# Two routed layers of a fused network: routes copied by DMA, shared rows first, an eviction moved, gating in smaller portions

## The chip, the cores and the metric

The kernel runs on 1 core of one Trainium2 chip. Its time is the device time of one execution in microseconds (us), the median of several runs. Five engines work side by side, each through its own queue in order: TensorE (PE; its weight loads are PEld), VectorE (DVE), ScalarE (ACT), GpSimd (POOL) and SyncE (SP, which here only issues DMAs). They wait for each other by semaphores.

## The reference

x is 16 batches x 256 tokens x 128 channels in float32, and passes through four pairs of sublayers, each added to its input: a cross attention and a feed-forward network, layers 0 to 3. Only two feed-forward networks change. With x normalised over its channels:

```python
# layer 1: 8 experts of 176 hidden units, the best 2 by score, and one shared expert
scores = softmax(x @ gate_w.T); idx = top_k(scores + gate_b, 2)
rw = zeros(T, 8).at[idx].add(scores[idx])
h  = silu((x @ w1[e] + b1[e]) * (x @ w3[e] + b3[e]))          # for each expert e
y  = sum_e rw[e] * (h @ w2[e] + b2[e])  +  the same of the shared expert, unweighted

# layer 2: 16 experts, all computed, weights rw from a gating with a softmax over the positive logits
q, k, v = (sum_e rw[e] * (x @ proj[e]) for the three projections)
ao  = softmax(causal(q @ k.T / sqrt(128))) @ v
out = sum_e rw[e] * (ao @ o_proj[e])
```

## The kernel before

The 4096 tokens lie in SBUF as x_sb. Each sublayer is a block with a barrier at its end. A feed-forward block runs 8 iterations (ITERS) of 512 tokens (T4); the first and last two are written out, the middle ones are a hardware loop of two iterations. Within a block the order of each engine's work is written out by hand; what an iteration prepares for the next (normalisation, transposes, gating: the functions named front_...) stands at fixed steps between the main work.

**Layer 1 (layer1_ffn).** The nine experts' 9 x 176 = 1584 hidden rows lie one behind the other and are cut into 13 chunks (CH) of 128 rows, the last of 48. At step k TensorE does the six one-pass matmuls of the next chunk (up, L1446; two products, each in three high and low parts), then front work, then the output matmul of the chunk two steps back (down, L1462, float32, two records), then spread (L1452): a bf16 matmul of a 0/1 matrix selb with the transposed routes rwTb, which puts into the psR bank the route of each hidden row. ScalarE adds a bias (L1380) and applies silu (L1386); VectorE multiplies the two products (L1567) and multiplies by psR (weigh, L1574). The biases of the output come by a separate matmul with the routes in float32 (L1460). For it the routes, with a constant 1 for the shared expert, are split by VectorE into three parts (three_parts, L1107 to L1112), transposed by TensorE (L1436) at step 11 and copied twice by ScalarE (L1374, L1375). No DMA is issued in this block. At its head GpSimd fills two tiles (L1355, L1356), for which VectorE and TensorE wait.

**Layer 2 (layer2_ffn).** The routes go to memory and come back spread over all partitions by DMA (L1733, L1739), four experts to a group. An iteration j (main) has 16 steps, one per expert: VectorE scales x by the route (L2037), ScalarE makes a rounded high part (xsh, L1809), VectorE the low part (xsl, L2041), TensorE nine matmuls (L1925). A ring of four tiles links them. Then come the attention and, mixed into it, 16 output matmuls (mix_o, L1913) for iteration j - 1. At the end of main ScalarE evicts their sum (store_o, L1804) and only then turns to the first high part of the next iteration. The gating of the next iteration is done by VectorE at steps 6 to 9 and 11, ScalarE's exponential stands at step 10, the transposed output (out_T) at 10, its addition at 12, the transposes of the routes (L1867) on TensorE at 14 and their copy (L1798) on ScalarE after step 15. In the first iteration the attention runs without output matmuls. In what follows a "seam" is the passage from one iteration to the next.

The order on ScalarE at the end of an iteration (store_o waits for the last output matmul) and at the start of the next:

```python
                if has_second_next(j):
                    front_squares(j + 2)
                if not is_first(j, 1):
                    store_o(j)
...
                    act.wait_ge(s("scaled").sem, s("scaled").at(qn(j, e + 1)))
                    nc.scalar.activation(xsh[:, e % RING, :], xs[:, e % RING, :], ACT.Copy)
```

## Time and profile before

| | |
|---|---|
| median of 3 runs | 1762.16 us (1762.01 to 1770.39) |
| the profiled execution | 1769.78 us, span 1767.8 us |
| busy share of the span | PE 86%, PEld 59%, DVE 69%, ACT 50%, POOL 10% |
| granted TensorE clock, mean | 0.945 of full speed |
| layer 1's feed-forward block | 436 to 740 us |
| layer 2's feed-forward block | 916 to 1440 us |
| DMA | 108 MB, 61 GB/s over the span |

One execution was profiled, on its only core. A line of the trace gives the start and the length of an instruction in us, its engine, its line in the kernel, its tiles and, in brackets, how long the engine was idle before it and what released it. Matmuls are pipelined: a record of 0.4 us may start every 0.23 us, so the distance between starts counts. Some matmul records are missing. Records of the same group that follow each other are merged (x14). PEclk is the clock that the throttle granted, 1.00 being 2.4 GHz.

### The profile page before, as it was taken

How to read it: one execution, taken by the hardware profiler on the slowest of the kernel's cores; microseconds unless marked ns; L12 is line 12 of the kernel's file. 1: busy time of each engine (PE TensorE's matmuls, PEld its weight loads, DVE VectorE, ACT ScalarE, POOL GpSimd, SP SyncE). 2: the span in 40 equal slices, each digit the busy share in tenths (PEclk: the TensorE clock that was granted, in tenths of full speed). 3: DMA queues.
4: the chain of work that ended last, by engine and by line, in shares of the span. 5: the costliest groups of instructions: out<-in, count | busy, mean ns of one | idle time of the engine just before them, and what ended most of it. 6: DMA issues, size and time to landing. Idle time of an engine off the chain costs nothing. (4 is left out here: it accounts for less than half of the span.)

```text
span 1767.8 us, 24778 instructions
## 1 busy us (share of the span) xinstructions
PE 1516.7 (86%) x8181; PEld 1038.8 (59%) x8201; DVE 1217.6 (69%) x2650; ACT 883.5 (50%) x1583; POOL 178.4 (10%) x171
## 2 busy tenths in 40 slices
PE   6999988896899999988966899999999988979407
PEld 5777765554566666566644656656656745655206
DVE  3888965786676676556656576767666557877896
ACT  2656644774556555465632333232233227756893
POOL 2111011130000000111410000000000011121000
PEclk9999999999899999999987999999999999999758
DMA  4000001320000000051202342433244312100001
GB/s 170 1 1 1 0 1 37 116 55 19 1 0 1 0 0 1 9 171 49 59 8 96 136 151 108 156 144 134 105 167 167 123 64 70 50 24 1 1 0 48
DMA packets 33708, 108.03 MB, mean 61 GB/s; under 512 B 8957, under 2 KB 12413, under 8 KB 24638
## 3 DMA queue, kind: packets, MB, share of 16 engines
q1 hardware_dynamic: 33598, 106.64, 17.9%
q8 instruction: 59, 0.97, 0.2%
q14 instruction: 51, 0.42, 0.1%
HBM read 85.38 MB, written 2.36 MB: 50 GB/s over the span
## 5 line engine op out<-in xcount | busy, mean ns | idle before, releaser
L1016 DVE TENSOR_REDUCE mP_a<-psY_a 128x8 f32<-128x512 f32 x192 | 128.1, 688 | 102.1 <-PE psY_a L842 102.0
L760 ACT ACTIVATE probs_a<-psX_a 128x512 f32<-128x512 f32 x192 | 109.0, 595 | 129.1 <-PE psX_a L869 128.3
L1809 ACT ACTIVATE xsh_f<-xs_f 128x512 fp32r<-128x512 f32 x128 | 79.4, 630 | 166.8 <-DVE xs_f L2037 166.8
L1567 DVE SCALAR_TENSOR_TENSOR g_f<-psU_f,cols_f1w,t_f 128x512 f32<-128x512 f32 (+1 forms) x104 | 77.9, 749 | 72.8 <-ACT t_f L1380 71.0
L1913 PE MATMUL psX_f<-xs_f,wo_f2w 128*128 128x512 f32 x256 | 121.3, 606 | 2.1 <-DVE xs_f L2037 1.5
L1380 ACT ACTIVATE t_f<-psU_f,cols_f1w 128x512 f32<-128x512 f32 (+1 forms) x104 | 71.1, 684 | 76.2 <-PE psU_f L1446 76.2
L1462 PE MATMUL psO_f<-h_f,w_f1w 128*128 128x512 f32 (+1 forms) x208 | 107.6, 599 | 0.0
L2041 DVE TENSOR_TENSOR xsl_f<-xs_f,xsh_f 128x512 fp32r<-128x512 f32 x128 | 87.8, 686 | 16.0 <-ACT xsh_f L1809 14.9
L842 PE MATMUL psY_a<-ks_a,xs_a 96*128 96x256 f32 x384 | 94.7, 348 | 4.1 <-DMA xs_a<-ql_a 2.4
L869 PE MATMUL psX_a<-xs_a,ks_a 128*128 128x256 f32 x384 | 86.2, 325 | 13.3 <-ACT xs_a L749 13.3
L1023 DVE RECIPROCAL heads_a<-psV_a 128x256 f32<-128x256 f32 x48 | 83.9, 1748 | 8.8 <-PE psV_a L882 8.8
L1925 PE MATMUL psQ_f<-xsh_f,wql_f2w 128*128 128x512 f32 x128 | 58.8, 459 | 35.1 <-DVE xsl_f L2041 34.7
L2268 PE MATMUL ps_f<-sel 128*128 128x512 f32 x76 | 23.1, 452 | 72.4 <-DVE gt_f L2495 72.4
L842 PEld LDWEIGHTS psY_a<-ks_a,xs_a 96*128 96x128 f32 x384 | 64.2, 199 | 34.2 <-DVE mP_a L1016 22.8
L869 PEld LDWEIGHTS psX_a<-xs_a,ks_a 128*128 128x128 f32 x384 | 63.4, 195 | 28.0 <-ACT xs_a L749 24.6
L1574 DVE TENSOR_TENSOR h_f<-act_h_f,psR_f 128x512 f32<-128x512 f32 (+1 forms) x104 | 70.5, 678 | 13.5 <-ACT act_h_f L1386 8.7
L183 POOL TENSOR_TENSOR rstd_f<-vareps_f,mhalf 128x4 f32<-128x4 f32 x16 | 18.1, 1133 | 562.1 <-DVE vareps_f L169 562.1
L1913 PEld LDWEIGHTS psX_f<-xs_f,wo_f2w 128*128 128x128 f32 x256 | 45.0, 192 | 48.8 <-issue 29.9
L1386 ACT ACTIVATE act_h_f<-g_f 128x512 f32<-128x512 f32 (+1 forms) x104 | 65.0, 625 | 3.2 <-DVE g_f L1567 3.1
L469 PE MATMUL psC_a<-vhat_a,pT_a 128*128 128x128 f32 x512 | 63.2, 277 | 0.5 <-DVE x_sb L546 0.5
L469 PEld LDWEIGHTS psC_a<-vhat_a,pT_a 128*128 128x128 f32 x512 | 61.2, 194 | 1.3 <-issue 0.6
L2268 PEld LDWEIGHTS ps_f<-sel 128*128 128x128 f32 x76 | 15.9, 221 | 76.4 <-issue 73.2
(444 smaller groups left out, 3969.5 us busy)
## 6 DMA issues: line engine op xcount, KB each, us to landing
wq_f2w<-f_routes SPq DMA_DIRECT2D x16, 1024.0 KB, 4.6
wk_f2w<-f_routes SPq DMA_DIRECT2D x16, 1024.0 KB, 4.7
wv_f2w<-f_routes SPq DMA_DIRECT2D x16, 1024.0 KB, 4.7
ring_f2w<-f_routes SPq DMA_DIRECT2D x16, 1024.0 KB, 4.8
xs_a<-qh_a SPq DMA_DIRECT2D x168, 64.0 KB, 2.0
xs_a<-ql_a SPq DMA_DIRECT2D x84, 64.0 KB, 2.0
xs_a<-probs_a SPq DMA_DIRECT2D x36, 64.0 KB, 2.0
x_sb<-in_x SPq DMA_DIRECT2D x1, 2048.0 KB, 8.0
```

Source lines behind the costliest of these rows:

```text
L469: ins = nc.tensor.matmul(psC[:, 0:P], pT[:, g % 2, k * P:(k + 1) * P], vhat[:, g // TPI % 2, g % TPI // 2, k, :], start=k == 0, stop=k == ...
L760: nc.scalar.activation(probs[:, b % 2, g, :, :], psX[g % 2][:].rearrange("p (e t) -> p e t", e=2), ACT.Exp, scale=float(dv) ** -0.5).then_ ...
L842: ins = nc.tensor.matmul(psY[h % 2][:, e * GK:(e + 1) * GK], xs[0:MAXROW, j % 2, g, t:t + P], ks[0:MAXROW, j % 2, p, g, :], start=not mask ...
L869: ins = nc.tensor.matmul(psX[g % 2][:, e * ST:(e + 1) * ST], ks[:, j % 2, p, g, e * P:(e + 1) * P], xs[:, j % 2, g, p * ST:(p + 1) * ST], ...
L1016: nc.vector.tensor_reduce(mP[:, b % 2, h // 2, col:col + 8], psY[h % 2][:].rearrange("p (h k) -> p h k", h=8), axis=AX.X, op=ALU.max).then ...
L1023: nc.vector.reciprocal(heads[:, b % 2, :], psV[:, ST:2 * ST]).then_inc(s("sums_inverted").sem, 1)
L1380: nc.scalar.activation(t3[r, g % 2, :], psU[g % 2][r, 1, :], ACT.Identity, bias=cols[r, CH + g % CH:CH + g % CH + 1])\
L1462: ins = nc.tensor.matmul(psO[:], w2[0:rows[k], k, :], h[0:rows[k], g % 2, :], start=False, stop=k == CH - 1)
L1567: nc.vector.scalar_tensor_tensor(g_[r, g % 2, :], psU[g % 2][r, 0, :], cols[r, k:k + 1], t3[r, g % 2, :], ALU.add, ALU.mult).then_inc(s("h ...
L1809: nc.scalar.activation(xsh[:, e % RING, :], xs[:, e % RING, :], ACT.Copy).then_inc(s("x_high").sem, 1)
L1913: nc.tensor.matmul(psX[:], wo[:, e, :], xs[:, e % RING, :], start=e == 0, stop=e == E - 1)\
L2041: nc.vector.tensor_tensor(xsl[:, e % RING, :], xs[:, e % RING, :], xsh[:, e % RING, :], ALU.subtract)\
```

## The change

Layer 1. The 176 shared rows come first, as chunks of 128 and 48 rows (L1_ROUTED = 2), which need no route; 8 chunks of 128 rows of one expert each follow, and 3 chunks with 16 rows of each of the 8 experts. The selection matrix, its conversion to bf16 at the end of the attention before, the spread matmuls and the psR banks go. The route of each row comes from memory: SyncE writes the transposed routes and reads them back into spread0, spread1 (four experts each, over all partitions) and spread2 (16 partitions for each expert). The output biases become rows 64 to 72 of chunk 1's weights, and the routes rows 64 to 72 of its right side hs, so the bias matmul and the split into three parts go. The transposes of the routes move from step 11 to 10.

Layer 2. store_o moves behind the high parts of experts 0 and 1 of the next iteration; the gating goes from steps 6 to 9 and 11 to steps 7 to 11 and 13, one of its portions cut in two; the exponential moves from 10 to 12, out_T from 10 to 12, the addition from 12 to 14, the transposes of the routes from 14 to 15. Filler matmuls (keep_busy, one pass, 512 columns, from the constant sel into psX) are added in the prologue and between the parts of the first attention.

The diff, without the semaphores' counts and the host's reordering of the weights:

```diff
@@ -1291,49 +1291,60 @@
...
+L1_ROUTED = 2
+L1_BIAS_ROW = 64
...
+def layer1_rows():
...
+    first = [(L1_E, h) for h in range(L1_H)]
+    whole = [(e, h) for e in range(L1_E) for h in range(P)]
+    rest = [(e, P + 16 * c + i) for c in range(3) for e in range(L1_E) for i in range(16)]
+    return first + whole + rest
...
 def layer1_ffn(pr, x_sb, common, wt):
...
     T4 = TPI * P
+    routes = nc.dram_tensor("f1_routes", (ITERS, E * T4), F32).ap()
...
         top, gs = sb("top", [P, TPI]), sb("gs", [P, TPI])
-        rw, rest = sb("rw", [P, TPI, NE]), sb("rest", [P, TPI, NE])
-        hi, mid = sb("hi", [P, TPI, NE], BF16), sb("mid", [P, TPI, NE], BF16)
-        parts = sb("parts", [P, TPI, P])
-        rwT, rwTb = sb("rwT", [P, 2, T4]), sb("rwTb", [P, 2, T4], BF16)
+        rw, hs = sb("rw", [P, TPI, P]), sb("hs", [P, 2, T4])
+        spread = [sb("spread0", [P, 4 * T4]), sb("spread1", [P, 4 * T4]), sb("spread2", [P, T4])]
+        biases = slice(L1_BIAS_ROW, L1_BIAS_ROW + NE)
...
         psU = [ctx.enter_context(nc.psum_tensor(f"psU{k}_f1", [P, 2, T4], F32)) for k in range(2)]
-        psR = [ctx.enter_context(nc.psum_tensor(f"psR{k}_f1", [P, T4], F32)) for k in range(2)]
...
         psM = ctx.enter_context(nc.psum_tensor("psM_f1", [P, T4], F32))
-        NST = LN_STEPS + 1 + 1 + 1 + 1 + 1 + 5 + 1 + 5 + 1 + 1 + 3
-        rows = [min(P, L1_ALL - k * P) for k in range(CH)]
+        NST = LN_STEPS + 1 + 1 + 1 + 1 + 1 + 5 + 1 + 5 + 1
+        rows = [P, L1_H - P] + [P] * (CH - L1_ROUTED)
+        starts = [sum(rows[:k]) for k in range(CH)]
+        RC = CH - L1_ROUTED
...
@@ -1350,10 +1361,30 @@
+        @block.sync
+        def _(sp):
+            for j in range(ITERS):
+                sp.wait_ge(s("gate_parts").sem, s("gate_parts").at(j + 1))
+                sp.dma_start(routes[j].rearrange("(e t) -> e t", e=E), hs[L1_BIAS_ROW:L1_BIAS_ROW + E, j % 2, :])\
+                    .then_inc(s("routes_kept").sem, 16)
+                sp.wait_ge(s("routes_kept").sem, s("routes_kept").at(16 * (j + 1)))
+                for half in range(2):
+                    if j:
+                        sp.wait_ge(s("hidden_ready").sem, s("hidden_ready").at(RC * (j - 1) + 4 * (half + 1)))
+                    sp.dma_start(spread[half][:], routes[j, half * 4 * T4:(half + 1) * 4 * T4].partition_broadcast(P))\
+                        .then_inc(s(f"spread{half}").sem, 16)
+                if j:
+                    sp.wait_ge(s("hidden_ready").sem, s("hidden_ready").at(RC * j))
+                for e in range(E):
+                    sp.dma_start(spread[2][e * 16:(e + 1) * 16, :], routes[j, e * T4:(e + 1) * T4].partition_broadcast(16))\
+                        .then_inc(s("spread2").sem, 16)
...
         def _(pool):
-            nc.gpsimd.memset(rw[:], 1.0).then_inc(s("pool_steps").sem, 1)
-            nc.gpsimd.memset(parts[:], 0.0).then_inc(s("pool_steps").sem, 1)
+            nc.gpsimd.memset(rw[:], 0.0).then_inc(s("pool_steps").sem, 1)
+            nc.gpsimd.memset(hs[:], 0.0).then_inc(s("pool_steps").sem, 1)
+            pool.wait_ge(s("pool_steps").sem, s("pool_steps").at(2))
+            nc.gpsimd.memset(rw[:, :, L1_BIAS_ROW + E:L1_BIAS_ROW + NE], 1.0).then_inc(s("pool_steps").sem, 1)
...
@@ -1371,8 +1402,7 @@
                 act.wait_ge(s("gate_T").sem, s("gate_T").at(j + 1))
-                nc.scalar.activation(rwT[:, q, :], psM[:], ACT.Copy)
-                nc.scalar.activation(rwTb[:, q, :], psM[:], ACT.Copy).then_inc(s("gate_parts").sem, 1)
+                nc.scalar.activation(hs[biases, q, :], psM[biases, :], ACT.Copy).then_inc(s("gate_parts").sem, 1)
...
@@ -1381,12 +1411,15 @@
             def silu(n, g):
-                r = slice(0, rows[g % CH])
+                r, k = slice(0, rows[g % CH]), g % CH
                 act.wait_ge(s("hidden_mul").sem, s("hidden_mul").at(n + 1))
-                nc.scalar.activation(act_h[r, g % 2, :], g_[r, g % 2, :], ACT.Silu).then_inc(s("hidden_act").sem, 1)
+                if k < L1_ROUTED:
+                    act.wait_ge(s("hidden_down").sem, s("hidden_down").at(n - 1))
+                kept = (h[r, g % 2, :], hs[r, g // CH % 2, :])[k] if k < L1_ROUTED else act_h[r, g % 2, :]
+                nc.scalar.activation(kept, g_[r, g % 2, :], ACT.Silu).then_inc(s("hidden_act").sem, 1)
...
             def store_out(j):
-                act.wait_ge(s("ffn_out").sem, s("ffn_out").at(j + 1))
+                act.wait_ge(s("hidden_down").sem, s("hidden_down").at((j + 1) * CH))
...
@@ -1405,8 +1438,9 @@
                                 front_exp(j + 1)
-                            if k == 11:
+                            if k == 10:
                                 front_parts(j + 1, 1 - p)
+            act.wait_ge(s("pool_steps").sem, s("pool_steps").at(3))
...
@@ -1433,12 +1467,12 @@
                 for c in range(TPI):
-                    ins = nc.tensor.transpose(psM[:, c * P:(c + 1) * P], parts[:, c, :], ident[:])
+                    ins = nc.tensor.transpose(psM[:, c * P:(c + 1) * P], rw[:, c, :], ident[:])
...
                 k, q = g % CH, g // CH % 2
-                cs, r = slice(k * P, k * P + rows[k]), slice(0, rows[k])
+                cs, r = slice(starts[k], starts[k] + rows[k]), slice(0, rows[k])
...
@@ -1446,22 +1480,19 @@
-            def spread(n, g):
-                k, q = g % CH, g // CH
-                pe.wait_ge(s("hidden_ready").sem, s("hidden_ready").at(n - 1))
-                nc.tensor.matmul(psR[g % 2][0:rows[k], :], selb[:, k * P:k * P + rows[k]], rwTb[:, q, :], start=True, stop=True)\
-                    .then_inc(s("gate_bcast").sem, 1)
...
                 if k == 0:
...
                     pe.wait_ge(s("ffn_outT").sem, s("ffn_outT").at(j))
-                    nc.tensor.matmul(psO[:], b2[:], rwT[:, q, :], start=True, stop=False)
-                pe.wait_ge(s("hidden_ready").sem, s("hidden_ready").at(n + 1))
-                ins = nc.tensor.matmul(psO[:], w2[0:rows[k], k, :], h[0:rows[k], g % 2, :], start=False, stop=k == CH - 1)
-                if k == CH - 1:
-                    ins.then_inc(s("ffn_out").sem, 1)
+                if k == 1:
+                    pe.wait_ge(s("gate_parts").sem, s("gate_parts").at(j + 1))
+                if k < L1_ROUTED:
+                    pe.wait_ge(s("hidden_act").sem, s("hidden_act").at(n + 1))
+                else:
+                    pe.wait_ge(s("hidden_ready").sem, s("hidden_ready").at(RC * j + k - L1_ROUTED + 1))
+                r = slice(0, L1_BIAS_ROW + NE if k == 1 else P)
+                rhs = hs[r, q, :] if k == 1 else h[r, g % 2, :]
+                nc.tensor.matmul(psO[:], w2[r, k, :], rhs, start=k == 0, stop=k == CH - 1).then_inc(s("hidden_down").sem, 1)
...
@@ -1489,15 +1520,12 @@
                             out_T(j - 1)
-                        if front and k == 11:
+                        if front and k == 10:
...
                             down(n - 2, (g - 2) % BODY, j - 1 if k < 2 else j)
-                        if k == 0:
-                            pe.wait_ge(s("gate_parts").sem, s("gate_parts").at(j + 1))
-                        spread(n, g)
...
@@ -1556,8 +1584,7 @@
                 steps.done(nc.vector.tensor_tensor(oh[:], oh[:], oh2[:], ALU.add))
-                steps.done(nc.vector.tensor_tensor(rw[:, :, 0:E], oh[:], ex[:], ALU.mult))
-                three_parts(nc, steps, rw[:], parts[:], hi[:], rest[:], mid[:], NE).then_inc(s("gate_ready").sem, 1)
+                nc.vector.tensor_tensor(rw[:, :, L1_BIAS_ROW:L1_BIAS_ROW + E], oh[:], ex[:], ALU.mult).then_inc(s("gate_ready").sem, 1)
...
@@ -1567,11 +1594,16 @@
-            def weigh(n, g):
-                r = slice(0, rows[g % CH])
+            def weigh(n, g, j):
+                c = g % CH - L1_ROUTED
+                if c < 0:
+                    return
+                if c in (0, 4, 8):
+                    dve.wait_ge(s(f"spread{c // 4}").sem, s(f"spread{c // 4}").at((16 * E if c >= 8 else 16) * (j + 1)))
                 dve.wait_ge(s("hidden_act").sem, s("hidden_act").at(n + 1))
-                dve.wait_ge(s("gate_bcast").sem, s("gate_bcast").at(n + 1))
-                nc.vector.tensor_tensor(h[r, g % 2, :], act_h[r, g % 2, :], psR[g % 2][r, :], ALU.mult)\
+                dve.wait_ge(s("hidden_down").sem, s("hidden_down").at(n - 1))
+                weights = spread[2][:] if c >= 8 else spread[c // 4][:, c % 4 * T4:(c % 4 + 1) * T4]
+                nc.vector.tensor_tensor(h[:, g % 2, :], act_h[:, g % 2, :], weights, ALU.mult)\
...
@@ -1589,7 +1621,7 @@
                         if g or not first:
-                            weigh(n - 1, (g - 1) % BODY)
+                            weigh(n - 1, (g - 1) % BODY, j if k else j - 1)
...
@@ -1807,10 +1840,12 @@
                     nc.scalar.activation(xsh[:, e % RING, :], xs[:, e % RING, :], ACT.Copy).then_inc(s("x_high").sem, 1)
+                    if e == 1 and not is_first(j, 2):
+                        store_o(j - 1)
...
                             front_x(j + 1, 1 - q)
-                        elif e == 10:
+                        elif e == 12:
...
@@ -1833,14 +1868,13 @@
                     front_squares(j + 2)
-                if not is_first(j, 1):
-                    store_o(j)
...
             run_mains(act, main)
+            store_o(ITERS - 1)
...
@@ -1926,7 +1960,7 @@
                         pe.wait_ge(s("ao_ready").sem, s("ao_ready").at(j))
-                    if e == 10 and not is_first(j, 2):
+                    if e == 12 and not is_first(j, 2):
...
@@ -1935,7 +1969,7 @@
                             front_logits(j + 1, 1 - q)
-                        elif e == 14:
+                        elif e == 15:
...
@@ -1946,13 +1980,25 @@
                 if is_first(j, 1):
+                    keep_busy(8)
...
                         stage()
+                        keep_busy(6)
+                    keep_busy(14)
...
                     mix_o(j, stages)
...
+            def keep_busy(n):
...
+                for _ in range(n):
+                    nc.tensor.matmul(psX[:], common["sel"][:, 0, :], common["sel"][:, 0:4, :], start=True, stop=True)
+            keep_busy(16)
             front_x(0)
+            keep_busy(4)
             front_logits(0, 0)
+            keep_busy(24)
             front_parts(0)
+            keep_busy(36)
...
@@ -2007,10 +2053,12 @@
-            def front_second(steps):
+            def front_inactive(steps):
...
                 steps.done(nc.vector.scalar_tensor_tensor(lg[:], oh[:], -1e30, lg[:], ALU.mult, ALU.add))
...
+            def front_second(steps):
...
@@ -2075,19 +2123,21 @@
                         low_part(E * j + e - 1, e - 1)
-                    if e == 12 and not is_first(j, 2):
+                    if e == 14 and not is_first(j, 2):
...
                     if not is_last(j):
-                        if e == 6:
+                        if e == 7:
...
                             front_gate(j + 1, steps)
-                        elif e == 7:
+                        elif e == 8:
                             front_best(steps)
-                        elif e == 8:
+                        elif e == 9:
+                            front_inactive(steps)
+                        elif e == 10:
                             front_second(steps)
-                        elif e == 9:
+                        elif e == 11:
                             front_mask(steps)
-                        elif e == 11:
+                        elif e == 13:
```

## Rows read from the trace of the kernel before

**Rows 1.** busy time by stretch; per engine, PEclk, DMA share, GB/s

```profile
438.00:740.00 302.00, 292.26 (x1092) 183.05 (x1112) 201.77 (x531) 166.93 (x271) 8.06 (x8) 0.97 0.00 1
```

**Rows 2.** in order of time (start us, us, engine, line), ScalarE, two evictions

```profile
564.40 0.60 ACT L1391 ACTIVATE oT_f<-psO_f 128x512 f32<-128x512 f32 x1 [2.41 <-PE psO_f L1462]
...
600.44 0.60 ACT L1391 ACTIVATE oT_f<-psO_f 128x512 f32<-128x512 f32 x1 [2.40 <-PE psO_f L1462]
```

**Rows 3.** in order of time, TensorE, one chunk

```profile
576.28 0.38 PE L1452 MATMUL psR_f<-rwTb_f,selb_f1w 128*128 128x512 bf16 x1
...
576.73 0.39 PE L1446 MATMUL psU_f<-xl_f,w3h_f1w 128*128 128x512 f32 x1
...
576.96 0.39 PE L1446 MATMUL psU_f<-xh_f,w3h_f1w 128*128 128x512 f32 x1
...
578.74 0.38 PE L1452 MATMUL psR_f<-rwTb_f,selb_f1w 128*128 128x512 bf16 x1
```

**Rows 4.** in order of time, TensorE, chunk 0 of an iteration

```profile
566.27 1.02 PE L1460 MATMUL psO_f<-rwT_f,b_f1w 128*128 128x512 f32 x2
...
567.13 1.02 PE L1462 MATMUL psO_f<-h_f,w_f1w 128*128 128x512 f32 x2
```

**Rows 5.** in order of time, VectorE, the gating stretch, one iteration

```profile
578.74 0.69 DVE L1574 TENSOR_TENSOR h_f<-act_h_f,psR_f 128x512 f32<-128x512 f32 x1 [1.19 <-ACT act_h_f L1386]
...
587.78 0.18 DVE L1107 CAST hi_f<-rw_f 128x36 bf16<-128x36 f32 x1
...
588.73 0.75 DVE L1567 SCALAR_TENSOR_TENSOR g_f<-psU_f,cols_f1w,t_f 128x512 f32<-128x512 f32 x1
```

**Rows 6.** in order of time, the second layer's first routes, SyncE and VectorE

```profile
937.15 0.34 SPq L1733 DMA_DIRECT2D f_routes<-rwT_f  x1
...
943.06 1.29 DVE L2037 TENSOR_TENSOR xs_f<-xT_f,wq_f2w 128x512 f32<-128x512 f32 x2 [2.29 <-DMA wq_f2w<-f_routes]
```

**Rows 7.** in order of time, GpSimd, fills at the head of two stages

```profile
436.33 0.52 POOL L1356 MEMSET parts_f<- 128x512 f32 x1
...
740.57 0.95 POOL L688 MEMSET vs_a<- 128x1024 f32 x1
```

**Rows 8.** in order of time, the seam from second to third iteration, four engines

```profile
1050.84 6.17 PE L1913 MATMUL psX_f<-xs_f,wo_f2w 128*128 128x512 f32 x14
...
1055.09 1.29 DVE L2037 TENSOR_TENSOR xs_f<-xT_f,wq_f2w 128x512 f32<-128x512 f32 x2
...
1057.05 0.60 ACT L1804 ACTIVATE oT_f<-psX_f 128x512 f32<-128x512 f32 x1 [2.67 <-PE psX_f L1913]
...
1058.94 0.50 PE L1925 MATMUL psQ_f<-xsh_f,wql_f2w 128*128 128x512 f32 x1 [1.93 <-DVE xsl_f L2041]
```

**Rows 9.** in order of time, VectorE, the loop's back edge

```profile
1178.85 1.29 DVE L2037 TENSOR_TENSOR xs_f<-xT_f,wq_f2w 128x512 f32<-128x512 f32 x2 [2.71 <-PE psX_f L1913]
```

**Rows 10.** in order of time, TensorE, first three experts after a later seam

```profile
1242.23 0.69 PE L1925 MATMUL psQ_f<-xsh_f,wql_f2w 128*128 128x512 f32 x1 [2.01 <-DVE xsl_f L2041]
...
1245.98 0.40 PE L1925 MATMUL psQ_f<-xsh_f,wql_f2w 128*128 128x512 f32 x1
...
1248.08 0.40 PE L1925 MATMUL psQ_f<-xsh_f,wql_f2w 128*128 128x512 f32 x1
```

**Rows 11.** in order of time, TensorE, starts of experts 5 and 10

```profile
1070.79 0.48 PE L1925 MATMUL psQ_f<-xsh_f,wql_f2w 128*128 128x512 f32 x1
...
1083.34 0.40 PE L1925 MATMUL psQ_f<-xsh_f,wql_f2w 128*128 128x512 f32 x1
```

**Rows 12.** in order of time, ScalarE, the end of an iteration's experts

```profile
1035.57 0.59 ACT L1798 ACTIVATE rwT_f<-psM_f 16x512 f32<-16x512 f32 x1 [5.38 <-PE psM_f L1867]
...
1037.67 0.60 ACT L1818 ACTIVATE qkvT_f<-psQ_f 128x512 f32<-128x512 f32 x1 [1.51 <-PE psQ_f L1925]
```

**Rows 13.** busy time by stretch, two stretches of the second layer

```profile
945.20:948.90 3.70, 3.62 (x9) 2.88 (x10) 2.34 (x4) 1.26 (x2) 0.00 (x0) 0.51 1.00 421
...
997.60:1003.30 5.70, 5.68 (x13) 4.46 (x14) 3.57 (x6) 1.89 (x3) 0.00 (x0) 0.50 0.48 187
```

More of the change, by code:

```diff
@@ L2107, in _ @@
             front_best(steps)
+            front_inactive(steps)
             front_second(steps)
@@ L2651, in joined @@
         return np.concatenate([a, b[None]], axis=0)
+    experts, places = np.array(layer1_rows()).T
     def chunked(a):
         out = np.zeros((L1_CH * P, a.shape[1]), a.dtype)
[L2655 to L2656 removed]
+        out[:L1_H] = a[:L1_H]
+        out[L1_ROUTED * P:] = a[L1_H:]
+        return out
     for k in ("w1", "w3"):
[L2659 to L2661 removed]
+        d["F1_" + k] = np.ascontiguousarray(joined(f["L1_ffn_" + k], f["L1_ffn_s" + k])[experts, :, places].T)
+    w2 = chunked(joined(f["L1_ffn_w2"], f["L1_ffn_sw2"])[experts, places])
+    w2[P + L1_BIAS_ROW:P + L1_BIAS_ROW + L1_E + 1] = joined(f["L1_ffn_b2"], f["L1_ffn_sb2"])
+    d["F1_w2"] = rows(w2)
+    d["F1_cols"] = np.concatenate([rows(chunked(joined(f["L1_ffn_" + k], f["L1_ffn_s" + k])[experts, places][:, None]))[:, :, 0]
                                    for k in ("b1", "b3")], axis=1)
[L2663 to L2666 removed]
     d["F1_gw"], d["F1_gb"] = f["L1_ffn_gate_w"].T, f["L1_ffn_gate_b"]
[L2668 removed]
     d["desc16"] = np.arange(L2_E, 0, -1).astype(np.float32)
```

31 lines of the change are left out of this document (11 added, 20 removed).

## The prediction

> **What bounds the kernel now.** I read the table by stretch of time first, then the instructions in order of time of one iteration on each engine, then the waits at the seams. The first routed layer runs from 438 to 740 us. In it TensorE is busy 292 of 302 us at a mean granted clock of 0.97 of 2.4 GHz [rows 1]; the reader is to see that no other engine comes near this. Its period is 600.44 - 564.40 = 36.04 us per iteration [rows 2], 13 chunks each. So here a matmul taken away is time taken away, as long as VectorE keeps up. The second routed layer (916 to about 1440 us) is bound by TensorE inside its loops over 16 experts but stands still at seams: at the change from one iteration to the next, and in the stretch where VectorE does the gating. The rest of the kernel isn't touched, apart from a weight conversion on ScalarE behind work that VectorE still does.
>
> **First layer, what goes from TensorE.** The one-pass bf16 matmul that spreads a route goes, 13 per iteration. Its price is its slot in the stream, not its duration: from it to the second matmul of the next chunk is 576.73 - 576.28 = 0.45 us, a plain one takes 576.96 - 576.73 = 0.23, so its slot is 0.22 of the chunk's 578.74 - 576.28 = 2.46 us [rows 3]. 13 x 0.22 = 2.9 us. The separate bias matmul goes too: 567.13 - 566.27 = 0.86 us [rows 4]; its rows now ride in the chunk of the last 48 shared hidden rows, and that matmul has 512 columns whatever its rows. Together 3.7 us per iteration, 30 us over 8.
>
> Does VectorE keep up? It loses two of 13 multiplications by the route (0.68 each) and the three-part split, 588.73 - 587.78 = 0.95 us [rows 5]. It is unbroken from the multiplication at 578.74 on, and the matmuls of chunk 11 wait a little for it (about 0.3 us, twice). I set up the new iteration, with chunks 2.24 us apart: VectorE then ends the product of chunk 9 some 15.7 us after the start of chunk 5's matmuls, TensorE is there at 15.1. So one stall of 0.6 us where there are now three of about 0.2; net nothing. The transposes of the routes, now one step earlier (10 for 11), need the routes at that time + 1.5 and VectorE has them at + 1.0. The new waits: a multiplication by the route waits for the down matmul two chunks back; the product before it on VectorE ends about 0.7 us after that matmul, so this wait is covered, and was already there through the spread matmul. ScalarE's silu of chunk 1 waits for the last down matmul of the iteration before, some 0.2 us; queued behind it are the two copies of the next x, with 2 us to spare.
>
> **First layer, what is added.** One write of the routes to memory and 10 reads per iteration on SyncE's queue, which was empty in this layer. The same pair in the second layer takes 943.06 - 937.15 = 5.9 us from issue of the write to the first product with it [rows 6]. Here routes are on their way some 12 us before chunk 2 needs them (5 chunks of 2.24 us), so 6 us are to spare; the reads of the third piece (8 issues) have over 15 us. In the first iteration there is no lead: 5.9 us against some 8 us until chunk 2's product, which nothing covers if it is late, worth 0 to 2 us once; I take 0. At the head of the layer VectorE waits for three fills in place of two. 128x512 takes 0.52 us, 128x1024 0.95 [rows 7]; so 0.46 + 0.95 + 0.15 in place of 0.55, +1.0 us. Against this the split (0.95) and one of two copies on ScalarE (0.5) go from the same serial head: -0.5 in all. First layer: -30.5 us, bounds -20 (a stall of 1.3 us more per iteration) and -34 (all present stalls go).
>
> **Second layer, the output's eviction.** At a seam the last output matmul is issued until about 1056.9; ScalarE has waited for it and evicts at 1057.05, only then makes the high part of the first scaled x, VectorE the low part, and TensorE starts at 1058.94 after 1.93 us. Yet the scaled x was there at 1055.78 [rows 8]. With the eviction behind two high parts: high part 55.8 to 56.45, low part to 57.15, start at 57.2. That is 1.7 us less. There are 6 such seams (the first iteration has no output to evict, the last eviction stands after the loop as before); but at the loop's back edge VectorE itself comes only at 1178.85, after 2.7 us [rows 9], so that seam gains nothing: 5 x 1.7 = 8.5 us. What is late next is the last output matmul itself.
>
> The seams have a second price. After such an idle time the first expert takes 1245.98 - 1242.23 = 3.75 us where the next takes 2.10 [rows 10]: the granted clock has gone to its lower level, 1.2 GHz, with some 1.5 us lost. I found this at five of the six seams, one of them the back edge. With 0.3 us of idle time in place of 2 the clock should hold at the four others, 6 us at most, 0 at least; I take 4.
>
> **Second layer, gating in smaller portions.** From expert 5 to expert 10 the matmuls take 1083.34 - 1070.79 = 12.55 us in place of 5 x 2.10 = 10.5 [rows 11]: VectorE has 1.3 to 1.95 us of gating beside 1.2 us of its own per expert, more than 2.10 in two of them, and begins it by waiting for the logits. Begun one expert later, VectorE is an expert ahead when it waits, and no portion is over 1.3 us; by my sum it stays 0.5 to 1 us ahead of TensorE throughout. 2.0 us gone, 7 times (the last iteration has no gating to do). The addition, now at 14, keeps its stall of about 0.2. A price comes with it: the routes' transposes go behind expert 15's matmuls, so ScalarE copies them (0.49 between starts) after these and not 2.1 us before the q, k, v evictions [rows 12]. TensorE waits for that copy before the output matmuls, and scores wait for the evictions: +0.4 us. Net -1.6 x 7 = -11, bounds -6 and -14. SyncE's write of the routes is 0.8 us later, its reads have several us left.
>
> **Second layer, filler matmuls.** They show nowhere in this place in the trace, so both ends from rows. The granted clock is 0.51 in the first 3.7 us of the first iteration, and 0.50 for 5.7 us after the 5.6 us of idle time that follow the first attention [rows 13]. At the upper level a filler takes 0.23 us: 16 + 4 + 24 + 36 of them fit the waits within half a us each, and give back 1.8 us (9 matmuls, 0.2 each) and about 0.5 in the transposes. After the first attention, 8 + 5 x 6 + 14 delay the next iteration by 3.0 us (it could start at 997.6, the fillers and the chain through them end at about 1000.6) and give back 14 x 0.2 = 2.8. Sum: -2. At the lower level, 0.43 us each, the prologue is 14 us longer and the attention 13 more, +27 for the other end. I take -2: the engine is busy without a gap before each group but the first.
>
> **Sum.** Against the profiled run's own 1769.8 us (span 1767.8): -30.5 - 8.5 - 4 - 11 - 2 = -56, so 1714. That run lies 7.6 us above the median of the runs, 1762.2; the removed slots are the same in both, so I forecast 1762 - 56 = 1706 us.
>
> **Rivals.** (1) VectorE becomes the bound of the first layer's gating stretch. For: it has 12 us there without a gap [rows 5]. Against: it loses 0.95 + 0.68 of them. Costs 1.3 us x 8 = 10: 1716.
> (2) The fillers run at the lower clock, for the reason that the first of them start cold: +27 + 2, so 1735. Against: the clock rose in under 6 us of matmuls each time in [rows 10, 13].
> (3) The clock falls in the first layer's loop, where 0.6 us of idle time per iteration are now in one place. For: it falls after the seams. Against: 0.6 is a third of a seam's idle time, and at 36 us periods with three small stalls it held. Once per iteration at a seam's price, 8 x 1.5 = 12: 1718.
> The Trainium skill, TensorE: Matmul & The Clock Gate, section "A second HAM failure mode: psum-queue depth-cycling", says that frequent micro-idles between groups of matmuls that cycle through PSUM banks make the clock oscillate; this loop is of that kind. The trace of before doesn't bear it out for this layer, whose mean is 0.97 with its cold head included [rows 1]; hence the low chance of (3).
> (4) Slower than before: the spread routes arrive late in each iteration of the first layer, since SyncE serves write, two large and eight small reads in order and each waits for buffers to come free. VectorE stands at chunk 2, behind it the next product, behind that TensorE. Price: what the load takes over its 12 us of lead, x 8. It decides from 7 us of wait per iteration, a load of 19 us against 5.9 measured [rows 6]; with 8 us of wait, 1706 + 64 = 1770.
> (5) The layers gain nothing, as the freed slots are filled by another wait: 1762. Against it stands [rows 2, 3]: 13 x 2.46 plus the extra groups is the whole period.
>
> **How the numbers follow.** Forecast 0.66, (1) 0.14, (2) 0.07, (3) 0.06, (4) 0.04, (5) 0.03. The forecast's own range is 1698 to 1716. With (1), (3) and part of (2), and below it the upper bounds of the first layer (-3.5), the clock (-2) and the gating (-3) and some more for the 8 us by which runs differ, 1690 to 1726. About 0.5% (9 us) is what a measurement of this kernel can tell: faster 0.93, same 0.03, slower 0.04.
>
> **What would show it.** Right: eviction period in the first layer 32.3 us (+-0.5); no wait on SyncE's reads beyond the first iteration; second-layer seams of 0.3 us but one of 3; starts of experts 5 to 10 in 10.6 us; filler spacing 0.23. Wrong: VectorE waiting for a DMA at chunk 2, a granted clock under 0.95 between 460 and 700 us, filler spacing of 0.43, or a first-layer period over 33.5.

## The result

| | before | after |
|---|---|---|
| median of the runs, us | 1764.97 (4 runs, 1762.01 to 1770.39) | 1713.51 (4 runs, 1709.67 to 1718.13) |
| profiled run, its own time / span, us | 1769.78 / 1767.8 | 1713.01 / 1710.9 |
| ratio of the times | | 0.9691 [0.9664, 0.9719] |

The kernel is 3.1% faster. The forecast was 1714 us for the profiled run (measured 1713.0) and 1706 for the median (measured 1713.5, inside the range).

### The profile page after: what moved, and what is told of

Its sections match the earlier page's. It is cut to its first block and busy times, and to the rows that moved or that the text cites. A ratio compares the mean times of both kernels' runs of the same rounds, so it can differ in the third digit from the quotient of the medians.

```text
span 1710.9 us, 24871 instructions
## 1 busy us (share of the span) xinstructions
PE 1494.7 (87%) x8213; PEld 1042.7 (61%) x8213; DVE 1201.3 (70%) x2586; ACT 880.9 (51%) x1574; POOL 179.5 (10%) x172
## 5 line engine op out<-in xcount | busy, mean ns | idle before, releaser
L1594 DVE SCALAR_TENSOR_TENSOR g_f<-psU_f,cols_f1w,t_f 128x512 f32<-128x512 f32 (+1 forms) x104 | 78.0, 750 | 61.1 <-ACT t_f L1410 59.3
L1495 PE MATMUL psO_f<-h_f,w_f1w 128*128 128x512 f32 x192 | 98.4, 595 | 0.4 <-DVE h_f L1606 0.4
L1410 ACT ACTIVATE t_f<-psU_f,cols_f1w 128x512 f32<-128x512 f32 (+1 forms) x104 | 71.2, 685 | 52.8 <-PE psU_f L1480 52.1
L842 PEld LDWEIGHTS psY_a<-ks_a,xs_a 96*128 96x128 f32 x384 | 64.1, 198 | 32.3 <-DVE mP_a L1016 22.8
L1480 PE MATMUL psU_f<-xh_f,w3l_f1w 128*128 128x512 f32 (+1 forms) x104 | 75.3, 724 | 6.0 <-DVE g_f L1594 5.9
L1606 DVE TENSOR_TENSOR h_f<-act_h_f,spread_f 128x512 f32<-128x512 f32 x88 | 60.1, 683 | 10.9 <-ACT act_h_f L1419 8.3
L454 PE MATMUL psS_a<-khat_a,xT_a 128*128 128x512 f32 x128 | 60.1, 593 | 0.7 <-ACT khat_a L378 0.7
```

The source lines that it names most:

```text
L842: ins = nc.tensor.matmul(psY[h % 2][:, e * GK:(e + 1) * GK], xs[0:MAXROW, j % 2, g, t:t + P], ks[0:MAXROW, j % 2, p, g, :], start=not mask ...
L1480: ins = nc.tensor.matmul(psU[g % 2][r, half, :], wt_part[:, cs], x_part[:, q, :], start=m == 0, stop=m == 2)
L1495: nc.tensor.matmul(psO[:], w2[r, k, :], rhs, start=k == 0, stop=k == CH - 1).then_inc(s("hidden_down").sem, 1)
L1594: nc.vector.scalar_tensor_tensor(g_[r, g % 2, :], psU[g % 2][r, 0, :], cols[r, k:k + 1], t3[r, g % 2, :], ALU.add, ALU.mult).then_inc(s("h ...
```

## The profile after

**First routed layer.** The same view as in [rows 1], for the block from its first instruction to its last output eviction and a little beyond (before: 436.28 to 738.40, 302.1 us). Columns as there: length, busy time and count for TensorE, its weight loads, VectorE, ScalarE and GpSimd, granted clock, DMA share, GB/s.

```profile
437.97:712.65 274.68, 258.68 (x989) 169.52 (x989) 186.06 (x471) 165.36 (x263) 9.59 (x11) 0.98 0.19 70
```

It is 27.4 us shorter. The period shows in ScalarE's two evictions that answer to [rows 2]: 555.05 - 522.34 = 32.71 us in place of 36.04.

```profile
522.34 0.60 ACT L1424 ACTIVATE oT_f<-psO_f 128x512 f32<-128x512 f32 x1 [1.70 <-PE psO_f L1495]
...
555.05 0.60 ACT L1424 ACTIVATE oT_f<-psO_f 128x512 f32<-128x512 f32 x1 [1.64 <-PE psO_f L1495]
```

One of TensorE's waits is new. The view of waits, TensorE, that block (before, the first line stood at 5.8 and the second at 0.5):

```profile
PE psM_f L1458 <- DVE xn_f L175: 6.4, 1, 6.4
PE psU_f L1480 <- DVE g_f L1594: 5.9, 8, 0.8
```

Where one of the eight stands is seen in order of time. VectorE begins behind ScalarE's silu, is unbroken through the gating up to the product of 542.18, and TensorE's up matmuls start 0.77 us late:

```profile
534.84 0.69 DVE L1606 TENSOR_TENSOR h_f<-act_h_f,spread_f 128x512 f32<-128x512 f32 x1 [1.19 <-ACT act_h_f L1419]
...
541.87 0.19 DVE L1101 TENSOR_TENSOR oh_f<-desc_f1w,top_f 128x32 f32<-128x32 f32 x1
542.18 0.75 DVE L1594 SCALAR_TENSOR_TENSOR g_f<-psU_f,cols_f1w,t_f 128x512 f32<-128x512 f32 x1
```

```profile
536.02 0.60 PE L1500 MATMUL psM_f<-ident,oT_f 128*128 128x128 f32 x4
...
537.23 0.50 PE L1480 MATMUL psU_f<-xh_f,w3l_f1w 128*128 128x512 f32 x1
...
539.70 0.50 PE L1480 MATMUL psU_f<-xh_f,w3l_f1w 128*128 128x512 f32 x1
...
542.99 0.50 PE L1480 MATMUL psU_f<-xh_f,w3l_f1w 128*128 128x512 f32 x1 [0.77 <-DVE g_f L1594]
```

The four steps from 534.23 to the start at 545.38 take 11.15 us. They hold four chunks of 2.25 and two groups of transposes of 0.44 (536.46 - 536.02), 9.88 us; 1.27 us are lost there, in each iteration of the loop. No wait of VectorE for a DMA stands in the block.

VectorE needs 542.18 - 534.84 = 7.34 us from the start of this stretch to that product. Before the change it was 586.07 - 578.74 = 7.33 us ([rows 5] has the start): the three-part split stood behind this product and the two multiplications that went stand in other chunks, so nothing that was removed lay in these 7.3 us.

```profile
586.07 0.75 DVE L1567 SCALAR_TENSOR_TENSOR g_f<-psU_f,cols_f1w,t_f 128x512 f32<-128x512 f32 x1
```

At the layer's head the three fills of GpSimd that answer to [rows 7] take 1.6 us, as worked out:

```profile
437.97 0.53 POOL L1384 MEMSET rw_f<- 128x512 f32 x1 [39.42 <-POOLq L617]
438.43 0.95 POOL L1385 MEMSET hs_f<- 128x1024 f32 x1
439.44 0.11 POOL L1387 MEMSET rw_f<- 128x4 f32 x1
```

**Second routed layer, a seam** (in order of time; it answers to [rows 8, 10]). The eviction now stands behind two high parts and TensorE waits 0.35 us, not 2.01. The first expert takes 1085.16 - 1082.96 = 2.20 us, so the clock held.

```profile
1082.72 0.60 ACT L1837 ACTIVATE oT_f<-psX_f 128x512 f32<-128x512 f32 x1
...
1082.96 0.50 PE L1959 MATMUL psQ_f<-xsh_f,wql_f2w 128*128 128x512 f32 x1 [0.35 <-DVE xsl_f L2089]
```

**The back edge** (it answers to [rows 9]). Still an idle time of 2.84 us, and yet the first expert takes 1144.29 - 1142.09 = 2.20 us. Before it took 3.71 here.

```profile
1142.09 0.50 PE L1959 MATMUL psQ_f<-xsh_f,wql_f2w 128*128 128x512 f32 x1 [2.84 <-DVE xsl_f L2089]
...
1144.29 0.40 PE L1959 MATMUL psQ_f<-xsh_f,wql_f2w 128*128 128x512 f32 x1
```

**Gating.** Experts 5 to 10 take 1048.76 - 1038.16 = 10.60 us in place of 12.55 [rows 11], and ahead of the output matmuls stands the new wait for ScalarE's copy of the routes (before, the scores waited 0.81 us at this point for an eviction, now 0.23):

```profile
1038.16 0.48 PE L1959 MATMUL psQ_f<-xsh_f,wql_f2w 128*128 128x512 f32 x1
...
1048.76 0.39 PE L1959 MATMUL psQ_f<-xsh_f,wql_f2w 128*128 128x512 f32 x1
...
1063.53 1.12 PE L1947 MATMUL psX_f<-xs_f,wo_f2w 128*128 128x512 f32 x2 [0.84 <-ACT rwT_f L1831]
1064.89 0.49 PE L1922 MATMUL psQ_f<-qkvT_f 128*128 128x128 f32 x2 [0.23 <-ACT qkvT_f L1855]
```

**Fillers.** The first 16 of the prologue take 5.59 us: the granted clock is 0.50 from 895 to 898 us and 0.97 from 898 to 901. The last 36 run at 0.23 us each, the 20 behind the first attention at 0.24, and iteration 1 starts warm (at the upper level) right behind them:

```profile
894.59 5.59 PE L1994 MATMUL psX_f<-sel 128*128 128x512 f32 x16 [3.46 <-DVE simn_f L2016]
...
908.77 8.43 PE L1994 MATMUL psX_f<-sel 128*128 128x512 f32 x36
...
966.10 4.82 PE L1994 MATMUL psX_f<-sel 128*128 128x512 f32 x20
970.75 0.40 PE L1959 MATMUL psQ_f<-xsh_f,wql_f2w 128*128 128x512 f32 x1
```

**Where the 56.9 us of the two spans went.** First layer -27.4. Second layer (its first matmul to the next stage's first: 917.50 to 1441.12 before, 890.74 to 1384.56 after) -29.8. The rest +0.3, in which +1.7 is the work ahead of the first layer: in its last 18 us the mean granted clock was 0.79 (before 1.00).

## The experiments

Times are medians; "before" is the kernel before, run on the same chip beside each group. In the traces the stretches agree from kernel to kernel to about 0.1 us, while the whole times of one kernel differ by up to 15 us, so the stretches decide and the times only confirm. "Cold" is a stretch that begins at the lower level of TensorE's clock, "warm" one that begins at the upper.

**1. First layer alone.** The second layer as before the change.

> The first routed layer as changed, the second as before. My theory: the first layer's block gives 302.1 - 274.7 = 27.4 us by itself, whatever the second does, and the second's seams have their cold first experts (3.3 to 3.8 us) and its period of 60 to 62 us back: 1762 - 27 = 1735 us, ratio to before 0.984. The rival, that part of the gain credited to the second layer comes from a warmer start after the first: 1730 or less, and the second layer's first main starts warm.

Measured 1742.05 us, before 1773.98, ratio 0.9814 [0.9766, 0.9862]. The evictions of the first layer come at 521.74 and 554.45, 32.71 us apart as in the changed kernel, to the hundredth, and the second layer has its old periods (52.1, 61.2, 59.8, 62.6, 61.1, 60.1, 61.0 us). The two layers' gains are separate, and the second's first iteration starts cold (3.58): the rival fell. Of the six seams three are cold, where the kernel before had five and the expectation all.

**2. No fillers.**

```
-            keep_busy(16)
             front_x(0)
-            keep_busy(4)
             ... (likewise 24, 36; in the first attention 8, 6 per stage, 14)
```

> All filler matmuls of the second layer left out (they compute nothing that is used), the rest as changed. Mine: they only pay where they stand. The first attention gets 3.0 to 3.9 us shorter, the first experts of iterations 0 and 1 take 3.8 again (+1.6 and +1.9) and the transposes and logits of the prologue some 1 us more: within +-2 us of the changed kernel, 1712 to 1716 us, and the later seams stay warm (2.2 us). Rival: the fillers are what set the clock for the loop behind them, and without them the seams are cold again: +7, 1720.

Measured 1713.26, before 1773.98, ratio 0.9669 [0.9612, 0.9725]. Prologue and first two periods together take 28.29 + 50.98 + 57.31 = 136.58 us, in the changed kernel 27.47 + 52.54 + 55.57 = 135.58: the fillers are worth 1.0 us. The seams behind them with 0.35 us of idle time stay at 2.20; only the back edge took 2.93. They pay only where they stand.

**3. Eviction back at the end of an iteration.**

```
-                    if e == 1 and not is_first(j, 2):
-                        store_o(j - 1)
...
+                if not is_first(j, 1):
+                    store_o(j)
```

> Only the output's eviction put back to the end of an iteration, gating portions and fillers as changed. Both theories: seams of 2 us idle again, 5 x 1.7 = 8.5 us. Mine as forecast: an idle time of 2 us at the seam is what lets the clock fall, so four or five first experts take 3.3 to 3.8 us again, +6: 1714 + 14 = 1728 us. Rival, from the back edge of the changed kernel, where the clock held through 2.84 us of idle time: the idle time at the seam does not decide, what went before it does (the stalls of the gating stretch); all first experts take 2.2, 1722 us.

Measured 1725.11 (1723.44 to 1726.15), before 1773.98, ratio 0.9716 [0.9667, 0.9764]. All seams stand idle for 1.93 to 2.10 us again. But of the five only one is cold, with 3.75 us; at the next, the same idle time costs nothing more (1089.22 - 1087.01 = 2.21):

```profile
1027.16 0.66 PE L1958 MATMUL psQ_f<-xsh_f,wql_f2w 128*128 128x512 f32 x1 [1.93 <-DVE xsl_f L2088]
...
1030.91 0.40 PE L1958 MATMUL psQ_f<-xsh_f,wql_f2w 128*128 128x512 f32 x1
...
1087.01 0.50 PE L1958 MATMUL psQ_f<-xsh_f,wql_f2w 128*128 128x512 f32 x1 [2.01 <-DVE xsl_f L2088]
...
1089.22 0.40 PE L1958 MATMUL psQ_f<-xsh_f,wql_f2w 128*128 128x512 f32 x1
```

The back edge is cold too (3.48). Neither theory has it whole: after an idle time of 2 us the clock falls or it doesn't. More on this below.

**4. Gating back in its larger portions.** In the second layer VectorE's steps at 6, 7, 8, 9, 11 in place of 7 to 11 and 13, exp and output transposes at 10, addition at 12, routes' transposes behind expert 14.

> Only the gating of the second layer put back into its larger portions, the routes' transposes one expert earlier and the addition at 12; eviction behind two high parts and fillers as changed. Mine: experts 5 to 10 take 12.5 us again (+2.0), the wait of 0.84 us for the copy of the routes goes: +1.3 x 7 = +9, and all seams stay warm, since their idle time is 0.3 us: 1723 us. Rival: the stalls in the gating stretch are what lets the clock fall at the seam or at the back edge: first experts of 3.3 to 3.8 us at up to six seams, +9 more, 1732.

Measured 1728.09, before 1773.98, ratio 0.9728 [0.9678, 0.9778]. Experts 5 to 10 take 12.35 to 12.84 us again; an undisturbed period is 58.15 us in place of 56.64, so the smaller portions with their price are worth 1.5 us there (forecast 1.6). Over the seven periods it is 0.9 to 1.8 us each: from the first start of iteration 0 to that of iteration 7 the two kernels take 404.69 and 393.03 us, and of these 11.66 us 1.55 are the cold back edge, so 10.1 us are the portions'. The five seams of at most 0.45 us stay warm, the back edge took 3.76.

**5. Routes' transposes behind expert 14**, otherwise as changed. One number in the code: `elif e == 15` is 14 on TensorE.

> The changed kernel with one line of the second layer changed: the routes' transposes stand behind expert 14's matmuls again. Mine: the wait of 0.84 us (0.68 in two iterations) for ScalarE's copy before the output matmuls goes, and nothing takes its place, since VectorE has added and weighted by expert 14: period 55.8 in place of 56.65, 7 x 0.85 = -6: 1708 us by the changed kernel's 1713.5. Rival: the transposes, one expert earlier, wait for VectorE's addition at 14 in turn, and the period stays within 0.3 of 56.65: 1713.

Measured 1711.46, before 1766.42, ratio 0.9678 [0.9656, 0.97]. A period falls to 56.10 us, by 0.55 and not 0.85: the wait of 0.84 for the copy is gone, but the scores wait 0.81 us for ScalarE's evictions again, in place of 0.23. These two waits alone would leave 0.26; where the other 0.3 us come from is not shown. And at two places the clock fell where it held in the changed kernel, after the same idle time: at the back edge (3.00 us), and in the last 32 output matmuls, 15.67 us in place of 13.97. First the kernel with the earlier transposes:

```profile
1138.40 0.50 PE L1959 MATMUL psQ_f<-xsh_f,wql_f2w 128*128 128x512 f32 x1 [2.84 <-DVE xsl_f L2089]
...
1141.40 0.63 PE L1959 MATMUL psQ_f<-xsh_f,wql_f2w 128*128 128x512 f32 x1
...
1364.41 15.67 PE L1947 MATMUL psX_f<-xs_f,wo_f2w 128*128 128x512 f32 x32 [1.54 <-DVE xs_f L2085]
```

and the changed kernel at the second of the two places:

```profile
1368.06 13.97 PE L1947 MATMUL psX_f<-xs_f,wo_f2w 128*128 128x512 f32 x32 [1.54 <-DVE xs_f L2085]
```

**6. First layer: output transposes and addition behind the gating.**

```
-                        if k == 7 and not (first and p == 0):     (TensorE, out_T)
+                        if k == 11 and not (first and p == 0):
-                        if k == 8 and not (first and p == 0):     (VectorE, add)
+                        if k == 12 and not (first and p == 0):
```

> First layer only: the output's transposes moved from chunk 7 to 11 and the addition of 0.68 us on VectorE from chunk 8, inside the gating, to 12, behind it. Mine: VectorE's unbroken stretch is the cause of the one stall of 0.77 us per iteration, so the stall goes and the eviction period falls from 32.72 to 32.0 (down to 31.5 if the 0.2 us lost at chunk 9 goes too), 8 x 0.75 = -6: 1707.5 us. Rival: the loss comes from TensorE's own order (out transposes and small gaps between groups), not from VectorE; the period stays at 32.5 or more, 1712 or more.

Measured 1710.96, before 1766.42, ratio 0.9684 [0.9663, 0.9705]. The period is 32.53 us: 0.19 less, not 0.7. The stall of 0.77 shrank to 0.17, and the loss moved ahead: the step from chunk 7's up matmuls (535.95) to 538.94 takes 2.99 us although no transposes stand in it any more. VectorE's stretch is 0.6 us shorter (543.29 - 536.56 = 6.73 us up to the same product) and TensorE gains a third of it, so my theory that the stretch's length alone decides fell. ScalarE in order of time shows what begins late, an exp that waits for VectorE between two loads of a function table of 1.28 us:

```profile
531.52 1.28 ACT L1401 ACT_TABLE_LOAD   x1
533.78 0.23 ACT L1401 ACTIVATE ex_f<-lg_f 128x32 f32<-128x32 f32 x1 [0.97 <-DVE lg_f L1566]
...
534.60 1.28 ACT L1419 ACT_TABLE_LOAD   x1
535.90 0.63 ACT L1419 ACTIVATE act_h_f<-g_f 128x512 f32<-128x512 f32 x1
```

Only behind this silu can VectorE go on, after 1.19 us of waiting, and from there it is unbroken.

**7. Besides, VectorE's split of the next x moved from chunk 5 to 10.**

> The late addition of the first layer, and besides VectorE's split of the next x (0.69 us) moved from chunk 5, ahead of the gating's shift, to chunk 10. New theory: what delays VectorE is not how much it does in the gating stretch but when it can begin: ScalarE stands 0.97 us before its exp until VectorE has split and shifted, then loads its function table for the silu (1.28 us), and only then VectorE goes on. The shift comes 0.69 earlier, so the whole stretch does: period 31.9 in place of 32.53, 8 x 0.6 = -5 beside the late addition alone. Rival: VectorE's own sum in the stretch is the bound, as the prediction's first rival had it; the moved work is 0.69 ahead of the stretch and not in it, so the period stays within 0.1 of 32.5.

Measured 1705.07 (1704.27 to 1709.6), before 1768.69, ratio 0.9648 [0.9617, 0.9678]. ScalarE's exp waits 0.36 us in place of 0.97, and the period is 32.08 (the evictions at 519.43 and 551.50): 0.45 less where 0.6 was expected. The rival had none. So the start of the stretch counts, not only its length.

**8. The exp made a plain copy**, beside the late addition of experiment 6, so that no table is loaded. The kernel leaves out the softmax and gives wrong routes.

```
-                nc.scalar.activation(ex[:], lg[:], ACT.Exp)
+                nc.scalar.activation(ex[:], lg[:], ACT.Copy)
```

> The late addition of the first layer, and the gating's exp on ScalarE made a plain copy, so that no function table is loaded in the loop (the routes are then not the reference's). New theory: with both loads of 1.28 us and the wait between them gone VectorE starts its stretch 1.3 us or more earlier, and all that TensorE loses at chunks 7 to 10 (1.1 us) goes: period 31.4. Rival (VectorE's own sum): 32.4 or more. This bounds what any order of the gating could give.

Measured 1700.27, before 1768.69, ratio 0.9618 [0.9587, 0.965]. TensorE has no wait at all in the loop, and the period is

```profile
518.62 0.60 ACT L1424 ACTIVATE oT_f<-psO_f 128x512 f32<-128x512 f32 x1 [1.70 <-PE psO_f L1495]
...
550.04 0.60 ACT L1424 ACTIVATE oT_f<-psO_f 128x512 f32<-128x512 f32 x1 [1.64 <-PE psO_f L1495]
```

31.42 us, as expected. The changed kernel's 32.72 - 31.42 = 1.30 us is the loss of 1.27 counted above. Of it 0.19 is the late addition (experiment 6), and 32.53 - 31.42 = 1.11 us hang on the two table loads and the wait between them, which this run does not tell apart.

**9. Fillers moved behind the attention:** 8 before the scores, none between the stages, 24 at the end.

> The first attention of the second layer with 8 fillers before the scores and 24 behind the attention's last matmul, none between its stages; prologue as changed. Mine: without fillers in between the chain is as short as with none, 5.6 us of waiting behind it is filled, and iteration 1 starts warm: from the first start of iteration 0 to that of iteration 1 49.4 us in place of 52.5, the next period 55.6 as changed: -3, 1710.5. Rival: the clock falls already between the stages, the 24 fillers run at 0.43 us for their first part and end later than the 5.6 us: 51 us or more, no gain.

Measured 1708.03, before 1766.42, ratio 0.9671 [0.9651, 0.969]. From iteration 0 to 1 49.75 us in place of 52.54, iteration 1 warm (2.17), its period 55.63. The fillers between the stages did not keep any clock that mattered here; they made a chain longer that ScalarE and VectorE were waiting for.

```profile
957.58 1.50 PE L1936 MATMUL psM_f<-pT_f,v_f 128*128 128x128 f32 x12
...
964.75 0.47 PE L1959 MATMUL psQ_f<-xsh_f,wql_f2w 128*128 128x512 f32 x1 [0.19 <-DVE xsl_f L2088]
```

**10. Together.** Late addition, earlier transposes and moved fillers:

> The changed kernel with all three: late addition in the first layer, routes' transposes behind expert 14, fillers moved behind the attention. Mine: the three lie in different stretches and add: -6 -6 -3 = -15, 1698.5 us by the changed kernel's 1713.5, ratio to before 0.9615. Rival: what is gained comes back as a wait elsewhere, or the clock at the back edge falls: 1705 or more.

Measured 1706.75 (1700.8 to 1715.62), before 1766.42, ratio 0.967 [0.9643, 0.9698]. With the late split as well:

> The changed kernel with the late addition and late split in the first layer, the routes' transposes behind expert 14, and the fillers moved behind the attention. By the new theory 8 x 0.8 = 6.5 in the first layer, 3.5 from the transposes (0.5 x 7), 2.7 from the fillers: -12.5 beside the changed kernel, 1701 us, less 1 to 2 us where the clock falls at the back edge. Rival: the first layer gives 1.5 only: 1706.

Measured 1707.56 (1702.25 to 1717.35), before 1768.69, ratio 0.9662 [0.9631, 0.9692]. The stretches add as they should (32.53 and 32.09 in the first layer, 56.1 in the second, 48.9 for iteration 0), but both profiles are cold at the back edge (3.53, 3.57) and before the last output matmuls, which takes back 3.2 us of the 3.9 that the transposes give (7 x 0.55). Hence the last kernel, without the earlier transposes:

> The changed kernel with the late addition and late split in the first layer and the fillers moved, the routes' transposes left behind expert 15. If the earlier transposes are what makes the clock fall at the back edge and before the last output matmuls (cold in four of four profiles that have them, at 3.0 to 3.8 and 75.0 us, warm in the five that have neither them nor another seam idle of 2 us with fillers, at 2.2 and 73.3): both warm here, second layer's periods 49.7, 55.6, 56.6, 59.1, 56.6, 56.6, 55.9, first layer's 32.08: 1705 - 2.7 = 1702.5 us and below every kernel that has the transposes early. Rival: it is chance, by where in the run the seam falls; then one of the two places may be cold here too, 1704 or more.

Measured 1710.67 (1706.69 to 1714.37), before 1766.64, ratio 0.967 [0.9646, 0.9693]. Every stretch came as expected but one: the back edge was cold (3.02) after 3.03 us of idle time, the last output matmuls warm. So the earlier transposes are not needed to make it fall. Chance is left of my two accounts, but the 14 profiles show a tendency: in the six with the transposes behind expert 14 (before, experiments 1, 4, 5 and the first two of 10) the back edge is cold in 6 and the last output matmuls in 5, in the other eight in 3 and 1. Nothing here shows why. Of the kernels that leave nothing out that of experiment 7 has the lowest median, but its interval, [0.9617, 0.9678], still touches the changed kernel's, [0.9664, 0.9719]. A version that beats it beyond doubt was not found; the gains of 2.8 us (fillers) and about 4 us (addition and split: 222.10 to 218.15 us from the first layer's first eviction to its last) are shown by the stretches alone.

## Why the prediction was right, and where its sizes were off

**First layer, -30.5 forecast, -27.4 measured.** The removed matmuls gave what their slots said, and the routes by DMA cost nothing: no wait at any read, the first iteration included. The step that failed is "one stall of 0.6 us where there are now three of about 0.2; net nothing". The up matmuls of that chunk wait 0.77, and with what is lost at the chunks before it, it is 1.3 us per iteration. By the forecast's own slots (36.04 - 3.7 = 32.3) and the floor of experiment 8 (31.4) the kernel before lost 0.9. So 0.4 more per iteration, 8 x 0.4 = 3.2 us, a third of rival (1). The prediction set the removed 0.95 and 0.68 us against the stretch, but neither lies in it: 7.33 us before, 7.34 after, while TensorE comes to its end earlier by the spread slots that went (0.22 us a chunk). And the start of the stretch hangs on ScalarE's table loads and the wait between them (experiments 6 to 8), which stand in no term of the prediction. The head: fills +1.0 as worked out.

**Seams, -8.5 forecast, -9.0 measured** (five seams 1.93 to 2.10 to at most 0.35 us; the back edge 3.06 to 2.84, as forecast nearly nothing).

**Clock at the seams, -4 forecast, -7.7 measured.** All cold first experts went, 1.5 us at each of five. The forecast took four at a discount and left out the back edge, since its idle time stays; there the clock held in this profile (in nine of fourteen it fell), whether by chance or with the later transposes is not shown (experiment 10), so 1.5 of the 7.7 can't be put down to the change.

**Gating, -11 forecast.** Experts 5 to 10 gained 1.74 to 1.97 us, the waits behind them cost 0.4 more; by experiment 4 it is 10.1 in all. Right in mechanism and size, the price too: the new wait is 0.84, but 0.6 of it was there before as the scores' wait.

**Fillers, -2 forecast, -1.0 measured** (experiment 2). Only the first 8 or so ran at the lower clock, and rival (2), the lower clock throughout, fell. The prologue gave back 0.8 in itself and 1.6 at the warm start of iteration 0, as forecast (2.3). The term that was mis-sized is what the fillers of the attention give back, "14 x 0.2 = 2.8": experiment 2 and the changed kernel differ by 1.75 us in iteration 1 (34.59 and 32.84 from expert 0 to 15), against a delay of 3.2 (52.54 - 50.98, and the 1.6 of the cold start; forecast 3.0). Experiment 9 gets 2.8 of this delay back.

**The last iteration** gained 1.7 us that no step named: the last output matmuls ran at the upper clock, again without a cause that is shown. It is the same place that was cold in experiments 3, 4 and 5. Sum of the second layer: -9.0 - 7.7 - 10.1 - 1.0 - 1.7 = -29.5, measured -29.8, forecast -25.5; 0.3 us are not assigned.

**The median.** The two misses cancel (3 us less in the first layer, 4 more in the second), and the profiled runs differ by 56.8 us where 56 were forecast. Yet the median is 7.5 us above the forecast. The failing step is the carry-over: 56 us were taken off a median of three runs, 1762.2, while the difference had been read in a run at 1769.8. With a fourth run the median before is 1764.97, 2.8 us higher, and the medians differ by 51.5 us, 4.5 less than 56: the profiled run before lay 4.8 us above its median, the one after at its own. The kernel before had medians of 1774.0, 1766.4, 1768.7 and 1766.6 beside the experiments, on four chips, which fits a low draw of 1762.2, though the chip may have a share in it. That part of the 56 is the clock's luck in the two profiles is likely, and not shown for the other runs.

Rivals (3) to (5) fell: the granted clock from 460 to 700 us is 1.00, and the waits for reads that (4) needs aren't there.

The Trainium skill, TensorE: Matmul & The Clock Gate, section "A second HAM failure mode: psum-queue depth-cycling", which the prediction set beside rival (3): its oscillating clock isn't borne out here; a loop that stands still 0.77 us once and 0.2 to 0.3 us twice per 32.7 us keeps a granted clock of 1.00 from 460 to 700 us (0.98 with its cold head).

## To carry to other kernels

When work leaves an engine, ask first whether it stood inside the stretch for which another engine waits, and what the start of that stretch waits for: what was removed outside it doesn't shorten that wait. Fillers belong behind the last work that others wait for, in the idle time itself; between the stages they lengthened the chain here. Take a difference read in one profiled run off that run's own time, and give the median a spread of its own.

## What the chip showed that was not expected

After an idle time of about 2 or 3 us the fall of TensorE's clock is not certain. In the second layer, by the first expert's time (2.2 us warm, 2.9 to 3.8 cold) and by that of the last 32 output matmuls (13.97 us warm, 15.46 to 15.67 cold):

| idle time before | profiles | cold | warm |
|---|---|---|---|
| 0 to 0.45 us, five seams each | 11 | 0 | 55 |
| 0.78 and 1.54 us with four transposes between, before the last output matmuls | 14 | 6 | 8 |
| 1.93 to 2.10 us, five seams each | 3 (before, experiments 1, 3) | 7 | 8 |
| 2.80 to 3.10 us, the back edge | 14 | 9 | 5 |

The lower level is 1.2 of 2.4 GHz (granted clock 0.50 in [rows 13]), and a fall costs 1.5 to 1.7 us: with it the starts of experts 0 to 15 of the iteration behind the back edge span 35.21 us in experiments 2 and 10 (last kernel), without it 33.67. What decides between cold and warm at equal idle time stays open: neither the fillers, the gating's portions, the place of the eviction nor that of the routes' transposes settles it by itself, though the last goes with it (experiment 10). The spread between runs of one kernel goes with the mean granted clock, which fits such falls in the rest of the kernel too (not shown run by run): the second kernel of experiment 10 took 1702.25 us at 0.960 and 1717.35 at 0.950. For a kernel whose idle times are of this size a single profile can thus be off by 1.5 us at each of them.
